# Another order of the side work in layer 2 of a four-layer kernel

## The chip, the cores and the metric

The kernel runs on one core of a Trainium2 chip, in one launch. The metric is the device time of the execution in microseconds (us). The profile names the engines PE (TensorE), DVE (VectorE), ACT (ScalarE), POOL (GpSimd) and SP (SyncE, which only issues transfers here).

## The reference, cut to what matters

Sixteen sequences of 256 tokens with 128 features go through four layers. Each adds to `x` an attention-like branch and a feed-forward branch of the same normalised input. The change is in layer 2:

```python
xn = _layernorm(x)
x = x + _L2_attn_ref(xn, ...) + _L2_ffn_ref(xn, ...)

def _L2_attn_ref(h, Wq, Wk, Wv, Wf, bf, Wo):      # "wide": 16 heads of 8, forward and backward
    q, k, v = heads(h @ Wq.T), heads(h @ Wk.T), heads(h @ Wv.T)
    f = log_sigmoid(h @ Wf.T + bf)                 # gates, cumulated along the tokens
    o_fwd = forgetting_attn(q, k, v, f)            # causal, scores + gc[q] - gc[k]
    o_bwd = flip(forgetting_attn(flip(q), flip(k), flip(v), flip(f)))
    return concat(o_fwd, o_bwd) @ Wo.T

def _L2_ffn_ref(x, ...):                           # "local": two layers l = 0, 1
    for l in range(2):
        h = shift_token(x)
        q, k, v = split(h @ wqkv[l])               # 8 heads of 64
        q, k = rotary_xpos(l2norm(q) * qs, l2norm(k) * ks)
        x = x + local_attention(q, k, v) @ wo[l]   # windows of 64 tokens
        h = layernorm(shift_token(x)) * lg + lb
        a, g = split(h @ w1[l] + b1[l])
        x = x + (a * gelu(g)) @ w2[l] + b2[l]
    return x
```

## The kernel before

The four layers run one after the other, each over 16 batches of 256 tokens; `x_all` stays in SBUF. In layer 2 a round is one pass over 24 steps, listed in `ROUND`: steps 0 to 15 are pairs of heads of the wide attention, steps 16 to 23 are pairs of heads of the local attention, four for local layer 0 and four for layer 1. Every engine runs the same program `one(rd)` over these steps. At each step PE does the scores of the step's pair (masks at L230, products at L242, or L1328 and L1337 for local pairs), then the transposes of maxima (L1430) or probabilities (L1387), weighted values (L253, L1419) and sums (L1402). DVE takes the maxima (L261 and L262, or L1725), subtracts them from the queries (L1768, `l_qm`) and normalises the sums (L1740 and L1743, L1754 and L1757). ACT takes the exponentials (L1600, L1621).

Beside this stands the rest of the work, and `BESIDE` says which items of it follow at each step, in which order. All engines go through the same list:

- ahead, for the next batch: `stats` (DVE copies `x` and does bn_stats, L1780 to L137), `norm` (L147), `xnT`, `gates` and `cumulate` (L1443, L1453; DVE writes `l_cums` at L1799), `wide_k`, `wide_q` and `wide_v` (PE L1467, L1460, L1477);
- for each local layer l: `hand` (a copy on DVE, L1814 and L1818); `hT`, only for l = 1 (PE transposes `xl` at L1319, DVE copies it out at L1771 and L1772); `qk` l i, four blocks (PE L1497, ACT squares at L1658, DVE rotates and sums at L1833 to L1841, POOL takes the power at L1573 and multiplies at L1576); `qk_t` l i (PE transposes the block, ACT copies it); `v` l c (PE L1503, ACT L1661);
- `o` l half (PE transposes, ACT copies `l_oT`, L1671), `out` l (PE L1520), `shift` and `apply` (layer norm: DVE up to L137, POOL L142, DVE L147), `normed` l, `up` and `down`, and for the wide branch `wide_o` and `wide_out` (L1487).

An engine takes the items in the order of the list and waits in its own queue. On PE, `qk` 1, `v` 1 wait until DVE has copied `hT`, and `qk_t` waits for POOL's product:

```python
b = G.fill(pe, rd, item, [("hT", )] if l == 1 else [])
...
pe.wait_ge(qkn_ready[l], n * 4 + i + 1)
```

All items with a PSUM result share ring `G` of two banks in turn: a use waits until the reader of the use before the last has taken it. The scores have rings `A` and `B`, one double bank each: PE may fill `A` again when DVE's maxima are done. Transposes, values and sums have ring `C` of two banks.

A batch's work spreads over three rounds. Rounds 0 (before), 1 (start) and 2 (second) and the last two are unrolled, with the items whose batch doesn't exist left out; 14 rounds between are one loop, whose 13 turns go back to its first instruction. In the second round and in all 14 of the loop both the items ahead and those of local layer 1 are present. SP issues two copies (`v_half`) in each local layer after the second `v`.

Of the kernel before, what the change touches and what calls it, by code (L numbers as in the profile page):

```python
# [604 lines left out]
def layer1(nc, g, B):  # L605
# [424 lines left out]


BESIDE = {
    0: [("shift", 0), ("wide_o", 0), ("wide_o", 1)],
    1: [("apply", 0), ("wide_out", )],
    2: [("normed", 0), ("qk", 0, 0)],
    3: [("o", 1, 0), ("o", 1, 1), ("qk", 0, 1), ("up", 0, 0)],
    4: [("qk", 0, 2), ("out", 1)],
    5: [("up", 0, 1), ("up", 0, 2)],
    6: [("shift", 1), ("down", 0), ("apply", 1)],
# [1 line left out]
    8: [("qk_t", 0, 0), ("up", 1, 0), ("up", 1, 1)],  # L1041
    9: [("up", 1, 2), ("qk_t", 0, 1)],
    10: [("down", 1), ("qk_t", 0, 2), ("hand", 1)],
    11: [("hand", 0), ("hT", ), ("qk_t", 0, 3), ("stats", )],
    12: [("qk", 1, 0), ("norm", )],
    13: [("v", 0, 0), ("qk", 1, 1), ("v", 1, 0)],
    14: [("qk_t", 1, 0), ("v", 0, 1), ("xnT", )],
    15: [("qk", 1, 2), ("v", 1, 1)],
    16: [("gates", ), ("qk_t", 1, 1)],
    17: [("cumulate", ), ("wide_k", 0), ("qk", 1, 3), ("qk_t", 1, 2)],  # L1050
    18: [("wide_k", 1)],
    19: [("qk_t", 1, 3), ("wide_q", 0)],
    20: [("o", 0, 0)],
    21: [("wide_q", 1)],
    22: [("o", 0, 1)],
    23: [("out", 0), ("wide_v", )],
}
AHEAD = ("stats", "norm", "xnT", "gates", "cumulate", "wide_q", "wide_k", "wide_v")
FIRST = ("qk", "v", "qk_t", "hand", "local", "o", "out")
# [1475 lines left out]
```

## Time and profile before

| | |
|---|---|
| runs | 4224.95, 4216.50, 4222.96 us; median 4222.96 |
| profiled execution, its own time | 4224.95 us |
| its span in the profile | 4222.8 us |
| granted TensorE clock, mean over the span | 0.939 |
| layer 2 in the span | about 1316 to 3190 us |

The span is what the profile covers, from its first to its last record; about 2 us of the execution lie around it. The granted clock is a share of full speed. In the rows, a line names the source line, engine, operation, output and input tile; "x4" is a count of instructions, and a matmul of this kernel's f32 data shows as two. "[0.40 <-DVE l_cums L1799]" is idle time of the engine just before, and what ended it; "issue" is an end for which the profile shows no releaser.

### The profile page before, as it was taken

The numbers are of one execution on the slowest core, as the hardware profiler recorded it, in microseconds if no ns is written. First come the engines' busy times: TensorE is split into PE (matmuls) and PEld (weight loads), VectorE is DVE, ScalarE is ACT, GpSimd is POOL, SyncE is SP. The second block draws the span as 40 slices with busy tenths as digits, with TensorE's granted clock in tenths as the row PEclk, the third lists the DMA queues.
The fourth block names the chain that finished last, engine by engine and source line by source line (L and its number), as shares of the span: only waits on it lengthen the run. The fifth ranks groups of instructions, "written<-read, shape, count | busy, mean of one in ns | idle before, by whom it ended". The sixth has DMA issues, their size and how long they took to land. (4 is left out here: it accounts for less than half of the span.)

```text
span 4222.8 us, 86111 instructions
## 1 busy us (share of the span) xinstructions
PE 3817.7 (90%) x30766; PEld 2993.4 (71%) x30766; DVE 2775.5 (66%) x7915; ACT 1878.4 (44%) x3484; POOL 645.2 (15%) x736
## 2 busy tenths in 40 slices
PE   3677999999998999999999999999978998998988
PEld 3565777777775676666666666666657887888877
DVE  2554555555554666666666666666647888888888
ACT  0001222222222455555555555555545555555555
POOL 0000000000000122212211222222212222222222
PEclk8668999999998999999999999999989999999999
DMA  5000000000000000000000000000001000000000
GB/s 131 10 7 23 0 0 0 0 0 0 0 0 36 5 9 10 9 9 9 9 9 9 9 9 9 9 9 9 9 5 47 1 2 2 1 2 2 1 2 3
DMA packets 29333, 44.63 MB, mean 11 GB/s; under 512 B 5928, under 2 KB 20816, under 8 KB 28368
## 3 DMA queue, kind: packets, MB, share of 16 engines
q1 hardware_dynamic: 29136, 41.56, 3.9%
q8 instruction: 178, 2.92, 0.3%
q14 instruction: 19, 0.16, 0.0%
HBM read 24.38 MB, written 4.19 MB: 7 GB/s over the span
## 5 line engine op out<-in xcount | busy, mean ns | idle before, releaser
L242 PE MATMUL bank<-l_kT,l_qT 32*128 32x128 f32 (+1 forms) x3072 | 407.4, 360 | 1.1
L1600 ACT ACTIVATE l_probsT<-bank 128x768 f32<-128x768 f32 x256 | 207.6, 811 | 443.3 <-PE bank L242 442.5
L142 POOL TENSOR_TENSOR l_rstd<-l_var,w_neg_half 128x2 f32<-128x2 f32 (+1 forms) x92 | 67.4, 733 | 2044.0 <-DVE l_var L137 2044.0
L242 PE MATMUL bank<-l_qm,l_kT 32*128 32x128 f32 (+1 forms) x3072 | 371.2, 335 | 0.0
L1573 POOL TENSOR_TENSOR l_rinv<-l_ssm,w_neg_half 128x8 f32<-128x8 f32 x128 | 210.2, 1642 | 731.7 <-DVE l_ssm L1841 731.6
L261 DVE TENSOR_REDUCE l_negmax<-bank 128x2 f32<-128x256 f32 (+1 forms) x384 | 197.5, 514 | 185.6 <-PE bank L242 180.5
L242 PEld LDWEIGHTS bank<-l_kT,l_qT 32*128 32x128 f32 x3072 | 227.9, 192 | 88.5 <-issue 80.8
L859 ACT ACTIVATE l_probsT<-bank 128x768 f32<-128x768 f32 x128 | 103.4, 808 | 411.4 <-PE bank L242 411.4
L230 PE MATMUL bank<-masks,ident 128*128 128x256 bf16 x1536 | 248.9, 281 | 40.8 <-issue 32.3
L2021 PE MATMUL bank<-l_xnT,w_egate 128*128 128x256 f32 x1024 | 276.4, 394 | 0.0
L2021 PE MATMUL bank<-l_xnT,w_eup 128*128 128x256 f32 x1024 | 270.1, 387 | 0.0
L2033 PEld LDWEIGHTS bank<-w_edown,l_hT 128*128 128x128 f32 x2048 | 247.5, 192 | 21.3 <-issue 15.6
L2033 PE MATMUL bank<-w_edown,l_hT 128*128 128x128 f32 x2048 | 250.5, 276 | 13.0 <-DVE l_xt L2203 13.0
L774 PE MATMUL bank<-l_xnT,w_up 128*128 128x256 f32 x1024 | 258.1, 396 | 0.0
L786 PE MATMUL bank<-w_down,l_hT 128*128 128x128 f32 x2048 | 256.0, 280 | 0.0
L242 PEld LDWEIGHTS bank<-l_qm,l_kT 32*128 32x128 f32 x3072 | 240.5, 187 | 21.2 <-issue 9.9
L786 PEld LDWEIGHTS bank<-w_down,l_hT 128*128 128x128 f32 x2048 | 244.5, 196 | 0.0
L230 PEld LDWEIGHTS bank<-masks,ident 128*128 128x128 bf16 x1536 | 151.6, 101 | 116.9 <-issue 66.5
L262 DVE TENSOR_REDUCE l_negmax<-bank 128x2 f32<-128x512 f32 (+1 forms) x384 | 228.0, 594 | 0.0
L2021 PEld LDWEIGHTS bank<-l_xnT,w_egate 128*128 128x128 f32 x1024 | 203.9, 199 | 30.2
L2209 DVE RECIPROCAL l_rden<-l_den 128x256 f32<-128x256 f32 x128 | 223.4, 1745 | 0.6
L2021 PEld LDWEIGHTS bank<-l_xnT,w_eup 128*128 128x128 f32 x1024 | 201.8, 197 | 29.6
(308 smaller groups left out, 8567.1 us busy)
## 6 DMA issues: line engine op xcount, KB each, us to landing
l_v_half<-l_v SPq DMA_DIRECT2D x32, 264.0 KB, 3.2
l_v_half<-l_v SPq DMA_DIRECT2D x32, 132.0 KB, 3.1
x_all<-in_x SPq DMA_DIRECT2D x16, 128.0 KB
w_up<-in_up SPq DMA_DIRECT2D x1, 2048.0 KB
w_down<-in_down SPq DMA_DIRECT2D x1, 2048.0 KB
scratch<-l_y SPq DMA_DIRECT2D x128, 16.0 KB
w_egate<-in_egate SPq DMA_DIRECT2D x1, 2048.0 KB, 8.4
out_x<-x_all SPq DMA_DIRECT2D x16, 128.0 KB, 1.8
```

The lines of the kernel that those rows point to most:

```text
L230: pe.matmul(diagonal(two[:, i, 0:AW]), g.ident16[:, :], diagonal(mask[:, :]), start=True, stop=False, skip_group_check=True)
L242: lasts.append(pe.matmul(bank[:, at:at + n * P], lhs[:, c * P:(c + 1) * P], rhs[:, x0 * P:(x0 + n) * P], start=False, stop=(i == 1), skip_ ...
L261: dve.tensor_reduce(negmax[:, 0, :], two[:, :, 0:s], AX.X, ALU.max, negate=True)
L262: return dve.tensor_reduce(negmax[:, 1, :], two[:, :, s:AW], AX.X, ALU.max, negate=True)
L774: last = pe.matmul(b[:, j * S:(j + 1) * S], w["up1"][:, h:h + P], xnT[:, :], start=True, stop=True)
L786: last = pe.matmul(Db[:, c * P:(c + 1) * P], hT[:, e % 2, j, c * P:(c + 1) * P], w["down1"][:, e * HC + j, :], start=(j == 0), stop=(j == ...
L859: Bt.took(act.activation(probsT[:, (u // 2) % 2, 2 * (u % 2):2 * (u % 2) + 2, :], two[:, :, 0:AW], ACT.Exp), u)
L1573: pool.tensor_tensor(rinv[:, i, :], ssm[:, i, :], g.neg_half[:, 0:LH], ALU.pow).then_inc(rinv_ready[l], 1)
L1600: Bt.took(act.activation(probsT[:, (j // 2) % 2, 2 * (j % 2):2 * (j % 2) + 2, :], two[:, :, 0:AW], ACT.Exp), rd, use)
L2021: last = pe.matmul(b[:, j * S:(j + 1) * S], wt[:, h:h + P], xnT[:, :], start=True, stop=True)
L2033: last = pe.matmul(Db[:, c * P:(c + 1) * P], hT[:, e % 2, j, c * P:(c + 1) * P], w["edown3"][:, e * HC + j, :], start=(j == 0), stop=(j == ...
L2209: dve.reciprocal(rden[:, m % 2, :], den[:, m % 2, :]).then_inc(rden_ready, 1)
```

## The change

The table `BESIDE` is the only thing edited. The same items are done, some of them at other steps or in another order within a step. Items move for all engines at once.

```diff
 BESIDE = {
-    0: [("shift", 0), ("wide_o", 0), ("wide_o", 1)],
-    1: [("apply", 0), ("wide_out", )],
-    2: [("normed", 0), ("qk", 0, 0)],
-    3: [("o", 1, 0), ("o", 1, 1), ("qk", 0, 1), ("up", 0, 0)],
+    0: [("shift", 0), ("wide_o", 0), ("wide_o", 1), ("apply", 0)],
+    1: [("wide_out", ), ("normed", 0)],
+    2: [("qk", 0, 0), ("o", 1, 0)],
+    3: [("o", 1, 1), ("qk", 0, 1), ("up", 0, 0)],
     4: [("qk", 0, 2), ("out", 1)],
...
     10: [("down", 1), ("qk_t", 0, 2), ("hand", 1)],
-    11: [("hand", 0), ("hT", ), ("qk_t", 0, 3), ("stats", )],
-    12: [("qk", 1, 0), ("norm", )],
-    13: [("v", 0, 0), ("qk", 1, 1), ("v", 1, 0)],
-    14: [("qk_t", 1, 0), ("v", 0, 1), ("xnT", )],
-    15: [("qk", 1, 2), ("v", 1, 1)],
-    16: [("gates", ), ("qk_t", 1, 1)],
-    17: [("cumulate", ), ("wide_k", 0), ("qk", 1, 3), ("qk_t", 1, 2)],
-    18: [("wide_k", 1)],
-    19: [("qk_t", 1, 3), ("wide_q", 0)],
-    20: [("o", 0, 0)],
-    21: [("wide_q", 1)],
+    11: [("hand", 0), ("stats", ), ("hT", ), ("v", 1, 0), ("norm", )],
+    12: [("qk", 1, 0), ("v", 0, 0)],
+    13: [("v", 0, 1), ("qk", 1, 1), ("qk_t", 0, 3)],
+    14: [("qk_t", 1, 0), ("v", 1, 1), ("xnT", )],
+    15: [("qk", 1, 2), ("qk_t", 1, 1)],
+    16: [("gates", ), ("qk_t", 1, 2)],
+    17: [("cumulate", ), ("qk", 1, 3), ("wide_k", 0)],
+    18: [("wide_k", 1), ("wide_q", 0)],
+    19: [("qk_t", 1, 3), ("wide_q", 1)],
+    20: [("wide_v", )],
+    21: [("o", 0, 0)],
     22: [("o", 0, 1)],
-    23: [("out", 0), ("wide_v", )],
+    23: [("out", 0)],
 }
```

## Rows read from the trace of the kernel before

**Rows 1.** The page's part 1: busy time, share of the span, instructions
```profile
PE 3817.7 (90%) x30766; PEld 2993.4 (71%) x30766; DVE 2775.5 (66%) x7915; ACT 1878.4 (44%) x3484; POOL 645.2 (15%) x736
```

**Rows 2.** Busy time by rounds of layer 2's loop; PEclk is the granted clock
```profile
2192.95:2306.82 113.87, 110.12 (x1036) 78.35 (x1037) 73.70 (x210) 62.99 (x115) 23.56 (x19) 0.94 0.04 9
...
2419.06:2527.05 107.99, 104.14 (x1036) 74.43 (x1037) 73.44 (x210) 62.99 (x115) 23.57 (x19) 1.00 0.04 9
2861.02:2977.04 116.02, 111.85 (x1036) 79.44 (x1037) 73.69 (x210) 62.99 (x115) 23.56 (x19) 0.93 0.04 9
```

**Rows 3.** PE's waits from 1440 to 3060: us in total, times, longest
```profile
PE bank L230 <- issue: 32.3, 13, 2.9
PE bank L1467 <- DVE l_cums L1799: 5.6, 14, 0.4
...
PE bank L1497 <- ACT l_oT L1671: 3.5, 14, 0.3
```

**Rows 4.** Timeline of steps 1 and 2: start, duration, instruction
```profile
2424.74 0.68 DVE L262 TENSOR_REDUCE l_negmax<-bank 128x2 f32<-128x512 f32 x1
...
2426.27 0.60 PE L230 MATMUL bank<-masks,ident 128*128 128x256 bf16 x4
```

**Rows 5.** Timeline of step 11
```profile
2471.16 0.38 PE L1319 MATMUL bank<-w_ident,l_xl 128*128 128x128 f32 x2
...
2471.37 0.60 PE L1319 MATMUL bank<-w_ident,l_qk_raw 128*128 128x128 f32 x4
...
2472.24 0.41 DVE L1771 COPY l_hT<-bank 64x256 f32<-64x256 f32 x1
...
2472.67 0.43 DVE L1772 COPY l_hT<-bank 64x255 f32<-64x255 f32 x1
...
2473.12 0.29 DVE L1780 COPY l_xn<-x_all 128x256 f32 x1
...
2474.26 0.17 DVE L137 TENSOR_SCALAR l_var<-l_mean_var 128x2 f32<-128x2 f32 x1
```

**Rows 6.** Timeline of steps 15 and 16
```profile
2488.59 1.02 PE L1497 MATMUL bank<-w_qkv,l_hT 128*128 128x512 f32 x2
...
2489.45 1.02 PE L1503 MATMUL bank<-w_qkv,l_hT 128*128 128x512 f32 x2
...
2494.02 0.64 PE L1319 MATMUL bank<-w_ident,l_qk_raw 128*128 128x128 f32 x4
2494.82 1.04 POOL L1576 TENSOR_TENSOR l_qk_raw<-l_qk_raw,l_rinv 128x512 f32<-128x512 f32 x1
```

**Rows 7.** Timeline of PE in the last full round, step 14
```profile
3127.06 1.12 PE L1319 MATMUL bank<-w_ident,l_qk_raw 128*128 128x128 f32 x4 [3.56 <-POOL l_qk_raw L1576]
3127.97 1.92 PE L1497 MATMUL bank<-w_qkv,l_hT 128*128 128x512 f32 x2
```

**Rows 8.** Timeline of PE at one turn of layer 2's loop
```profile
2524.10 0.61 PE L1477 MATMUL bank<-w_v2w,l_xnT 128*128 128x128 f32 x4
2527.05 0.39 PE L230 MATMUL bank<-masks,ident 128*128 128x256 bf16 x2 [2.34 <-issue]
```

**Rows 9.** PE's longest waits in layer 1 and in layer 3
```profile
PE bank L764 <- DVE l_negmax L262: 33.9, 16, 2.1
...
PE bank L2009 <- DVE l_kv_junk L2185: 60.7, 15, 4.1
```

**Rows 10.** Busy time and granted clock of stretches just behind waits
```profile
434.37:437.80 3.43, 3.43 (x19) 3.37 (x20) 1.30 (x3) 0.00 (x0) 0.00 (x0) 0.59 0.00 0
554.89:558.30 3.41, 3.41 (x38) 2.89 (x38) 1.91 (x5) 0.00 (x0) 0.00 (x0) 1.00 0.00 0
3253.93:3257.34 3.41, 3.41 (x9) 2.78 (x10) 3.10 (x11) 1.50 (x4) 1.10 (x2) 0.57 0.00 0
3257.34:3260.75 3.41, 3.41 (x17) 2.97 (x17) 3.19 (x6) 2.58 (x5) 0.73 (x1) 0.93 0.00 0
2192.95:2205.45 12.50, 12.41 (x77) 8.85 (x77) 6.23 (x23) 0.60 (x1) 0.70 (x1) 0.50 0.01 3
```

## The prediction

> **What bounds the kernel now.** Read the page's busy shares first: TensorE (PE) is busy 90% of the 4222.8 us span, VectorE 66% and ScalarE 44% [rows 1]. The edited table is used by layer 2 only, and there by all engines, so second comes the table of busy time by round. A full round of the loop takes 107.99 to 116.02 us. PE is busy for all but about 4 us of each, and what sets long rounds apart is not work (x1036 matmuls in each) but the granted clock: 1.00 in the shortest, 0.94 and 0.93 in the others [rows 2]. Of the 13 rounds that end in a turn of the loop, three are short and ten long, over 111 us. Third, PE's waits in layer 2 [rows 3]: 32.3 us at the turn of the loop, where the profile shows no releaser ("issue"), then, among others, 5.6 for `l_cums` (14 times 0.40) and 3.5 for `l_oT` (14 times 0.25). So the order now hides nearly every answer of the other engines under matmuls. Anything that makes PE wait is paid in full, and a reordering can give back at most the few waits of this list.
>
> So each moved item needs one question: when PE comes to it at its new place, has the other engine answered? Below I take the times of the round from 2419.06 to 2527.05, all of it at full clock.
>
> **Step 0 to 3 (`apply` 0, `normed` 0, `o` 1 0 earlier).** `apply` is 0.59 us on VectorE (L147) and now runs before step 1's maxima. Those ended at 2425.42 (L262) and would end near 2426.3; PE's masks of step 2, which need the bank, start at 2426.27 and move to 2426.5, since `normed` (0.22 us of PE) comes ahead of them [rows 4]. It just fits: cost 0. It is the first place to turn into a wait if VectorE is late. In step 3 `qk` 0 1 needs the bank of `o` 1 0, which now stands a step ahead instead of just before: the 0.25 us for `l_oT` [rows 3] go. Gain 0.25 in 14 rounds, 3.5 us.
>
> **Step 11 (`stats` ahead of `hT`, `v` 1 0 directly behind it).** This is the largest term. Before, PE transposed `xl` 1 at 2471.16, went on at 2471.37 with `qk_t` 0 3 and the scores of step 12, and first needed `hT` for `qk` 1 0 at that step's end. VectorE copied `hT` from 2472.24 to 2473.10 and only then did the statistics, 2473.12 to 2474.43 [rows 5]. Now `v` 1 0 stands directly behind `hT` on PE and reads that copy, and on VectorE the statistics stand ahead of the copy. VectorE has other work until 2472.24; then 1.31 us of statistics (2474.43 less 2473.12), then 0.86 us of copies: 2474.41, and PE is there at 2471.37. Wait: 3.04 us and a few hundredths for the release, 3.1; 1.31 of it is the statistics' place, the rest the missing cover. Behind the waiting matmul stand all of PE's queue, step 12's scores first, and behind those VectorE's and ScalarE's next inputs; they only idle along. The second round and 14 rounds of the loop have both items: 15 x 3.1 = 46.5.
>
> **Steps 15 and 16 (`qk_t` 1 1 and 1 2 a step earlier).** After `qk` 1 2 comes a chain: ScalarE's square, VectorE's rotation and sums, GpSimd's power and its product, which ends at 2495.86. The matmul began at 2488.59, so a block can be transposed 7.27 us after it [rows 6]. `qk_t` 1 2 stood at the end of step 17; it now follows `gates` in step 16, where `qk_t` 1 1 stood, at 2494.02, 5.43 us behind 2488.59. On that way `qk_t` 1 1 takes the place of `v` 1 1: four transposes (0.42, twice the 0.21 from 2471.16 to 2471.37 in rows 5) for one product (0.86, from L1497 to L1503 in rows 6), so PE is there after 5.0 us. Wait: 7.27 - 5.0 = 2.3 us, 15 times: 34.5. `qk_t` 1 1 itself stays two steps behind its `qk` and doesn't wait. The last round has little beside this chain and waits up to 3.56 us for the same product already [rows 7]; there `qk` 1 3 is now held behind `qk_t` 1 2: by that row, +4.
>
> **Step 17.** `qk` 1 3 (0.86 us) now stands between `cumulate` and `wide_k` 0 and covers the 0.40 us wait for `l_cums` [rows 3]: -6.0 in 15 rounds.
>
> **`v`, `wide_q`, `qk_t` 0 3 and 1 3, `o` 0 0.** Same instructions, other steps. Their readers are two steps or more behind, and the two banks of ring G are freed by copies such as L1772 (0.43 us, rows 5) with a product of 0.86 us between: 0. SyncE's two copies per layer half are issued no later than before, and nothing stands behind them: 0.
>
> **`wide_v`, from the last place of the round to step 20.** It is 0.6 us of PE just ahead of the turn of the loop, where PE then idles 2.34 us [rows 8]. If the next pass can begin at a time that doesn't depend on it, those 0.6 us were covered and are now in the open (13 x 0.6 = 8); if the idle time simply follows PE's last matmul, 0. Nothing decides; I take 3.
>
> **The clock.** After the turn of the loop (2.5 us idle on average) the clock stood at 0.50 (1.2 GHz, the lower of its two levels; 1.00 is 2.4 GHz) for the next 12.5 us in the round from 2192.95, and that round took 5.88 us more than the one at 1.00 [rows 2, 10]. Layer 3 waits 15 times for about 4.05 us [rows 9], and after the first of these shows 0.57 and 0.93 in two pieces of 3.41 us: 3.41 x 0.43 + 3.41 x 0.07 = 1.7 us lost [rows 10]. Layer 1 waits 16 times for about 2.1 us [rows 9], and shows 0.59 after one of them and 1.00 after another [rows 10]. So each of the two new waits costs between 0 and 5.9 us beyond itself. For step 11, with dense 128-row matmuls behind it as in layer 3, I take 1.7 (26 in all). For step 16, a wait like layer 1's but with small matmuls behind it as at a round's start, I take 2.0 (30 in all).
>
> **Sum.** 46.5 + 34.5 + 4 - 3.5 - 6 + 3 + 26 + 30 = +134.5 us on the profiled execution's 4224.95, so 4360. That execution is the slowest of three, 2 us over their median of 4222.96; against the median I say 4358.
>
> Nearest to a reason against: could PE work past the waiting matmul? The last round shows it idle for 3.56 us at L1319 with L1497 next in line [rows 7]. The Trainium skill ("TensorE: Matmul & The Clock Gate", Part 2, the step on loading weights) says that only weight loads are pulled ahead while matmuls stay in program order. By that rule the 3.1 us stand in full and the sum is 4360; were it otherwise, step 12's scores would fill them and it would be 4360 - 46.5 - 26 = 4287. The trace agrees with the rule.
>
> **Rivals.**
> 1. Both waits come, but the clock stays at 1.00 behind them, as in most of layer 1's passes: 134.5 - 56 = +78.5, so 4302 against the median. Against it: layer 3's pass in rows 10, and ten of the 13 turns of the loop.
> 2. Both come, and each brings the long low clock of a round's start: 15 x 5.9 x 2 = 177 in place of 56, so 4479. For it: step 17's matmuls are as small as those of step 0. Against it: layer 3 recovers within 7 us.
> 3. Only one wait shows, because the other's chain is shorter than I read it: without step 16, 4358 - 34.5 - 30 = 4294; without step 11, 4285.
> 4. Faster: the waits removed count and the new ones don't, because VectorE reaches `hT` before PE. The gain is 9.5 us, 4213. With a shift of the loop's turn that left the clock up in the ten rounds that lose 5 us or so it would reach 4165. It decides at the `hT` copy: it would have to end by 2471.3 where it ends at 2473.10 even in the old order. I see no row for it.
> 5. The table changes order but the waits just take other waits' places, within 0.2%.
>
> **Chances.** My forecast (4325 to 4430) 0.50; rival 1, 0.17; rival 2, 0.10; rival 3, 0.13; rival 4, 0.06; rival 5, 0.04. About 0.2% (8 us) is what a measurement of this kernel can tell from no change. Faster 0.06, same 0.04, slower 0.90. For 8 in 10 the range goes from 4280 (rivals 1 and 3 inside) to 4440.
>
> **What would show it.** Among PE's waits: L1503 for VectorE's L1772, 15 times near 3.1 us; L1319 for GpSimd's L1576, 15 times near 2.3 us; no L1467 for L1799 and no L1497 for `l_oT`. By round: 5 us more of PE idle in each, and granted clock below 1.00 in all rounds, with low stretches in the middle of the round and in its last third. I am wrong if the first wait is near 1 us or absent, if PE's clock stays up behind the waits, or if the turn of the loop changes by more than 0.5 us.

## The result, and the profile after

The changed kernel is slower by 3.5%: its median is 4365.0 us (4 runs, 4362.1 to 4377.3) against 4219.7 us (4 runs, 4208.6 to 4225.0) for the kernel before on the same chip, a ratio of 1.0353 (95% interval 1.0324 to 1.0383). The prediction said 4358 us, 4280 to 4440, slower with a chance of 0.90. The profiled execution took 4374.6 us, its span 4372.6 us; the mean granted clock is 0.920.

The page's part 1 of the kernel after, the counterpart of [rows 1]:

```profile
PE 3893.2 (89%) x30766; PEld 3038.0 (69%) x30766; DVE 2780.6 (64%) x7915; ACT 1879.5 (43%) x3484; POOL 645.6 (15%) x736
```

The instructions are the same in number. PE shows 75.5 us more busy time for the same x30766 matmuls, and its weight loads (PEld) 44.6 us more, which is the first sign that its clock was lower; DVE, ACT and POOL show 5.1 us more at most. The rest of the 149.8 us by which the span grew is PE standing idle. Its waits in layer 2 of the kernel after say where (engine, line, what it waited for: us in total, times, longest), to be set against [rows 3]:

```profile
PE bank L1503 <- DVE l_hT L1772: 46.9, 15, 3.1
PE bank L1319 <- POOL l_qk_raw L1576: 34.7, 15, 2.3
PE bank L230 <- issue: 24.5, 13, 2.1
PE bank L1419 <- ACT l_probs2T L1607: 4.5, 8, 0.6
PE bank L1319 <- DVE w_rot L1850: 4.1, 14, 0.3
PE bank L1419 <- DVE l_on L1743: 3.9, 7, 0.6
```

Two waits lead the list that weren't in it, 15 times each, and L1467 for `l_cums` and L1497 for `l_oT` are gone. One round shows both. First step 11, from the timeline of the kernel after (start, duration, instruction, and in brackets the idle time ahead of it with its releaser); it answers to [rows 5]:

```profile
1827.41 0.38 PE L1319 MATMUL bank<-w_ident,l_xl 128*128 128x128 f32 x2
...
1828.74 0.29 DVE L1780 COPY l_xn<-x_all 128x256 f32 x1 [0.16 <-DVE l_xl L1818]
...
1829.88 0.17 DVE L137 TENSOR_SCALAR l_var<-l_mean_var 128x2 f32<-128x2 f32 x1
...
1830.38 0.43 DVE L1772 COPY l_hT<-bank 64x255 f32<-64x255 f32 x1
...
1830.93 2.07 PE L1503 MATMUL bank<-w_qkv,l_hT 128*128 128x512 f32 x2 [3.14 <-DVE l_hT L1772]
```

PE issues the transpose of `xl` 1 and stands until DVE has done the statistics (1828.74 to 1829.96, when the first copy starts) and the two copies. The first product behind the wait takes 2.07 us where this kind took 1.02 us in [rows 6]: the clock is already down. Then steps 15 and 16 of the same round, from the timeline of all engines, which answers to [rows 6]:

```profile
1853.42 1.02 PE L1497 MATMUL bank<-w_qkv,l_hT 128*128 128x512 f32 x2
...
1858.00 1.64 POOL L1573 TENSOR_TENSOR l_rinv<-l_ssm,w_neg_half 128x8 f32<-128x8 f32 x1 [5.99 <-DVE l_ssm L1841]
...
1859.71 1.04 POOL L1576 TENSOR_TENSOR l_qk_raw<-l_qk_raw,l_rinv 128x512 f32<-128x512 f32 x1
...
1860.89 0.47 PE L1319 MATMUL bank<-w_ident,l_qk_raw 128*128 128x128 f32 x1 [2.31 <-POOL l_qk_raw L1576]
```

From the product of `qk` 1 2 (1853.42) to its transpose (1860.89) are 7.47 us, of which PE had work for about 5. By rounds the kernel after takes from 116.4 to 123.0 us. Here are a short round and a long one (the columns are those of [rows 2]: the stretch, its length, busy us of PE, PEld, DVE, ACT and POOL, the granted clock, DMA share and GB/s):

```profile
1659.25:1775.67 116.42, 108.15 (x1036) 76.93 (x1037) 73.88 (x210) 63.01 (x115) 23.54 (x19) 0.96 0.04 8
1775.67:1898.30 122.63, 114.49 (x1037) 80.99 (x1037) 73.96 (x210) 63.01 (x115) 23.54 (x19) 0.90 0.03 8
...
1775.67:1788.17 12.50, 12.20 (x122) 8.98 (x124) 9.45 (x31) 2.49 (x4) 0.70 (x1) 1.00 0.01 3
...
1829.80:1840.00 10.20, 9.06 (x42) 4.80 (x43) 3.01 (x9) 1.80 (x3) 0.70 (x1) 0.51 0.00 0
...
1860.50:1874.20 13.70, 13.31 (x63) 10.06 (x64) 3.81 (x12) 6.11 (x11) 0.26 (x1) 0.51 0.00 0
```

The last three rows are pieces of the round from 1775.67. The clock is at full speed behind the turn of the loop, falls at the wait of step 11, comes back (1.00 from 1848 to 1858), and falls again at the wait of step 16. Over the 12 rounds between turns, the stretch at the lower level (1.2 GHz) behind step 11 is 10.2 us long in eight and 3.4 us in four; behind step 16 it is 13.7 us in ten and 6.8 us in two. Behind none of the 13 turns is there one, although PE idles 1.88 us there on average. Before, ten of the 13 had one.

What a microsecond of the lower level costs follows from the first two rows: the long round has 13.7 us more of it (10.2 + 13.7 against 3.4 + 6.8) and is 6.2 us longer, 0.45 us for each. The first two rounds of [rows 2] give about the same: 5.88 us for a stretch of 13.7 us, 0.43 us for each.

### The profile page after: what moved, and what is told of

Its sections match the earlier page's. It is cut to its first block and busy times, and to the rows that moved or that the text cites. A ratio compares the mean times of both kernels' runs of the same rounds, so it can differ in the third digit from the quotient of the medians.

```text
span 4372.6 us, 86070 instructions
## 1 busy us (share of the span) xinstructions
PE 3893.2 (89%) x30766; PEld 3038.0 (69%) x30766; DVE 2780.6 (64%) x7915; ACT 1879.5 (43%) x3484; POOL 645.6 (15%) x736
## 5 line engine op out<-in xcount | busy, mean ns | idle before, releaser
L242 PE MATMUL bank<-l_qm,l_kT 32*128 32x128 f32 (+1 forms) x3072 | 388.6, 348 | 0.0
L242 PEld LDWEIGHTS bank<-l_qm,l_kT 32*128 32x128 f32 x3072 | 250.9, 196 | 25.4 <-issue 12.9
```

What stands on the lines that cost most here:

```text
L242: lasts.append(pe.matmul(bank[:, at:at + n * P], lhs[:, c * P:(c + 1) * P], rhs[:, x0 * P:(x0 + n) * P], start=False, stop=(i == 1), skip_ ...
```

## The experiments

Each one edits `BESIDE` of the kernel after or of the kernel before. Times are medians, ratios are to the kernel before on the same chip.

### Each wait taken away, and both

Without step 11's: `hT` ahead of `stats`, and `v` 1 0 two steps later, at the kernel after.

```diff
-    11: [("hand", 0), ("stats", ), ("hT", ), ("v", 1, 0), ("norm", )],
-    12: [("qk", 1, 0), ("v", 0, 0)],
-    13: [("v", 0, 1), ("qk", 1, 1), ("qk_t", 0, 3)],
+    11: [("hand", 0), ("hT", ), ("stats", )],
+    12: [("qk", 1, 0), ("v", 0, 0), ("norm", )],
+    13: [("qk_t", 0, 3), ("v", 0, 1), ("qk", 1, 1), ("v", 1, 0)],
```

> The changed kernel with step 11 put right: statistics behind the hT copy, v 1 0 back in step 13. Theory (each new wait costs itself and a stretch at half clock behind it): the 3.14 us wait at L1503 is gone, the 2.31 us wait at L1319 stays. By the changed kernel's rounds a microsecond at the low clock costs some 0.42 us (122.4 us with 23.9 us low, 116.4 with 10.2), so a round is some 107 + 2.3 + 5.7 (13.7 us low) = 115 us and the time about 4255. Rival (the low clock is something each round has once, wherever it falls): the stretch behind the second wait stays, and another comes back at the turn of the loop, 119 us a round and 4300.

Measured: 4252.5 us, 1.0103 (1.0081 to 1.0125). The first of its waits of PE in layer 2:

```profile
PE bank L1319 <- POOL l_qk_raw L1576: 32.3, 14, 2.3
PE bank L230 <- issue: 21.4, 13, 2.1
```

A usual round in its table of busy time by rounds:

```profile
1639.52:1752.60 113.08, 108.40 (x1036) 77.70 (x1037) 73.77 (x210) 62.87 (x115) 23.57 (x19) 0.95 0.04 9
```

The wait of step 16 stays in full (14 of its 15 lie in this window), with 3.4 to 13.7 us of low clock behind it each time. Behind the turn there is one low stretch in 12 rounds.

Without step 16's: `qk_t` 1 1 and 1 2 back, at the kernel after.

```diff
-    15: [("qk", 1, 2), ("qk_t", 1, 1)],
-    16: [("gates", ), ("qk_t", 1, 2)],
+    15: [("qk", 1, 2)],
+    16: [("gates", ), ("qk_t", 1, 1)],
     17: [("cumulate", ), ("qk", 1, 3), ("wide_k", 0)],
-    18: [("wide_k", 1), ("wide_q", 0)],
+    18: [("qk_t", 1, 2), ("wide_k", 1), ("wide_q", 0)],
```

> The changed kernel with qk_t 1 1 in step 16 and qk_t 1 2 in step 18, so that the chain of qk 1 2 is covered again; step 11 as changed. Theory: the 2.31 us wait is gone, the 3.14 us wait stays, with 3.4 to 10.2 us at the low clock behind it: 107 + 3.1 + 1.4 to 4.3 = 111.5 to 114.5 us a round, 4215 to 4250. Rival (low clock once per round at any place): also a low stretch at the turn of the loop, 117 to 119 us a round, near 4290.

Measured: 4309.8 us, 1.0242 (1.0217 to 1.0268). From its waits of PE:

```profile
PE bank L1503 <- DVE l_hT L1772: 43.8, 14, 3.1
...
PE bank L1453 <- DVE l_ze L1794: 4.7, 14, 0.3
PE bank L242 <- DVE l_qm L1768: 2.9, 14, 0.3
```

From its busy time by stretches, one of the shortest rounds and the first 10.2 us of the next:

```profile
1638.74:1754.71 115.97, 110.04 (x1036) 78.04 (x1037) 73.85 (x210) 62.71 (x115) 23.51 (x19) 0.94 0.04 8
1754.71:1764.91 10.20, 10.11 (x70) 7.13 (x71) 6.01 (x22) 0.60 (x1) 0.70 (x1) 0.55 0.01 2
```

This missed what my theory gave (4215 to 4250 us) and came nearer to its rival, low clock at the turn again and 4290 us. The wait is gone, but the low stretch at the round's start is there in all 12 rounds (10.2 or 13.7 us), though PE idles no longer at the turn than in the kernel after (1.78 us). So the clock took back much of what the wait gave. Two waits of 0.3 and 0.2 us are new as well.

Without both, the two edits together:

> Both put right, all other moves of the change kept. Theory: none of the two waits, l_cums and l_oT waits still gone, the turn of the loop idle for some 1.9 us as in the changed kernel, in place of 2.5. If the low clock at a round's start came with the longer idle time, it stays away: 107 us a round, 4150. If it only stayed away because the two waits had shifted it, it is back in most rounds: 111 us a round, 4205. Rival on the prediction (the other moves cost something too): above 4220.

Measured: 4188.5 us, 0.9942 (0.9919 to 0.9964), which is 0.6% faster than the kernel before. That lies between the two times expected, 4150 with no low start and 4205 with most. The longest of its waits of PE in layer 2's loop is the turn:

```profile
PE bank L230 <- issue: 20.6, 13, 1.7
```

Two of its rounds, one behind the other (five of 12 have a low start):

```profile
1744.27:1851.26 106.99, 103.96 (x1036) 74.20 (x1037) 73.50 (x210) 62.82 (x115) 23.60 (x19) 1.00 0.04 9
1851.26:1962.58 111.32, 108.46 (x1037) 77.51 (x1037) 73.76 (x210) 62.81 (x115) 23.59 (x19) 0.95 0.04 9
```

The whole loss is in these two waits and what hangs on them. In shares of the time before: undoing step 11 gives back 3.53% - 1.03% = 2.50% (105 us), step 16 1.11% (47 us), both 4.11% (173 us). The waits themselves are 46.9 and 34.7 us, and the last round's for POOL's product grow by 9.0 us besides (the table below); without both edits of the change they are back at 9.1 us in total, as before (9.3). The two effects don't add up (152 against 173), because with one of them gone the low clock sits elsewhere in the round.

### Half a wait

`hT` ahead of `stats`, with `v` 1 0 left where the change puts it, at the kernel after:

```diff
-    11: [("hand", 0), ("stats", ), ("hT", ), ("v", 1, 0), ("norm", )],
+    11: [("hand", 0), ("hT", ), ("stats", ), ("v", 1, 0), ("norm", )],
```

> The changed kernel with hT ahead of the statistics in step 11 again, v 1 0 still directly behind them on TensorE. It parts the 3.14 us wait: the statistics' place is worth 1.31 us, the missing cover the rest. Theory: the wait at L1503 is 3.14 - 1.31 = 1.8 us, 15 times, -20 us; whether the clock still falls behind a wait of 1.8 us decides between 4345 (it does, with stretches as before) and 4290 (it doesn't, 4 to 5 us less in each round). Rival (the wait is a fixed cost of putting v 1 0 behind hT): near 3.1 us and 4365.

Measured: 4323.7 us, 1.0252 (1.0230 to 1.0275). The first of its waits of PE:

```profile
PE bank L1319 <- POOL l_qk_raw L1576: 32.3, 14, 2.3
PE bank L1503 <- DVE l_hT L1772: 23.6, 14, 1.7
```

The wait shrinks from 3.14 to 1.69 us, by the statistics' 1.31 and a little more. Behind it the clock is low in only four of 12 rounds, where it was in all. Four rounds have a low start.

`v` 1 1 between `qk` 1 2 and its transpose again, at the kernel after:

```diff
-    14: [("qk_t", 1, 0), ("v", 1, 1), ("xnT", )],
+    14: [("qk_t", 1, 0), ("xnT", )],
     15: [("qk", 1, 2), ("qk_t", 1, 1)],
-    16: [("gates", ), ("qk_t", 1, 2)],
+    16: [("v", 1, 1), ("gates", ), ("qk_t", 1, 2)],
```

> The changed kernel with v 1 1 moved from step 14 to the head of step 16, ahead of gates: 0.86 us more of TensorE work between qk 1 2 and qk_t 1 2, nothing else. Theory: the wait at L1319 for GpSimd's product falls from 2.31 to 1.45 us, -13 us; if the low stretch behind it (13.7 us in most rounds) stays, 4352; if a wait of 1.45 us leaves the clock up, some 5 us less per round and 4275. Rival (the chain of qk 1 2 itself is held up by something in step 16): the wait stays near 2.3 us.

Measured: 4316.4 us, 1.0236 (1.0216 to 1.0257). From its waits of PE:

```profile
PE bank L1319 <- POOL l_qk_raw L1576: 18.1, 13, 1.4
```

From its table by rounds the longest, with low stretches behind the turn and both waits:

```profile
2832.44:2959.50 127.06, 119.71 (x1037) 84.53 (x1037) 74.25 (x210) 62.77 (x115) 23.54 (x19) 0.87 0.03 8
```

One product of 0.86 us as cover shortens the wait from 2.31 to 1.4 us, by 0.9. Behind it the clock stays up in nine of 12 rounds. The start is low in four. So waits of 1.4 and 1.7 us sometimes lower the clock, and waits of 2.31 and 3.14 us did each time.

### The place of `wide_v`

`wide_v` alone, at the kernel before:

```diff
-    20: [("o", 0, 0)],
+    20: [("wide_v", ), ("o", 0, 0)],
...
-    23: [("out", 0), ("wide_v", )],
+    23: [("out", 0)],
```

> The kernel before with one edit: wide_v from the end of step 23 to step 20. The prediction gave this move 0 to +8 us. The changed kernel's turns of the loop are idle for 1.9 us on average, not 2.5. If wide_v's move does that: turns near 1.9, 4212, and if the low clock needs the longer idle time, down to 4160. If the move has nothing to do with it: turns near 2.5 and 4220 to 4228.

Measured: 4206.6 us, 0.9990 (0.9978 to 1.0003). Within what can be told from no change: `wide_v`'s 0.6 us, 13 times, would be a ratio of 1.0019. PE's idle time at the turn is 26.9 us in total (2.07 on average) where before had 32.3, so it is nearer to the 1.9 us that I expected if the move shortens it than to 2.5. The other way round, `wide_v` last in the version without both waits:

```diff
-    20: [("wide_v", )],
+    20: [],
...
-    23: [("out", 0)],
+    23: [("out", 0), ("wide_v", )],
```

> The kernel with both waits put right (turn of the loop idle 1.58 us on average), with wide_v back at the end of step 23. If wide_v's place sets the idle time at the turn (code for the next pass is asked for later when more work stands ahead of it): turns near 2.0 to 2.5 us, more low starts, 4200 to 4215. If it doesn't (the idle time follows the last matmul, and its size is that of the loop's code in memory): turns stay near 1.6 us and 4185 to 4190.

Measured: 4195.8 us, 0.9959 (0.9942 to 0.9976); the idle time at the turn stays at 21.6 us in total (20.6 with `wide_v` in step 20). So `wide_v` covers nothing there. Whether its place has a part in the shorter idle time of the kernel after isn't settled: moving it at the kernel before took 5.4 of the 7.8 us away, moving it back here gave only 1.0 us back.

### The turn of the loop, with the code moved

Another candidate is where the instructions lie in the program. These two put 128 waits that are already satisfied once ahead of layer 2 on PE's queue, which moves the loop in the program (lines of their profiles are two higher behind it).

```diff
             pe.wait_ge(setup_done, 1)
+            for _ in range(128):
+                pe.wait_ge(setup_done, 1)
```

At the kernel before:

> The kernel before, with 128 waits that are already satisfied put on TensorE's queue once, ahead of layer 2's first round. The order of work is untouched; only the place of the loop's code in memory moves. So far turns of the loop idle 1.6 to 1.9 us on average in all runs whose page counts 166 packets on the instruction queue, with wide_v last or not; 2.1 us with 169, 2.5 us with 178 (the kernel before). Theory (the idle time at the turn is a matter of where the code lies): the number of packets changes and the turns with it, down to 1.6 us, 12 us less in all, or up; plus up to 5 us for the waits themselves. 4200 if it falls. Rival (the turn depends on the order of work): 2.5 us, 178 packets, 4215 to 4220.

At the kernel after:

> The changed kernel with the same 128 waits. By the same theory its turns of 1.9 us may change too (to 2.5 us if the packets go back to 178: +8 us, 4373); the two waits of 3.14 and 2.31 us can't change, nor the low stretches behind them. Rival: 1.9 us and 4365 to 4370.

Measured: 4222.5 us, 0.9992 (0.9979 to 1.0004), and 4366.0 us, 1.0346 (1.0327 to 1.0365): neither moves. The idle time at the turn is 2.35 us on average (2.48 before) and 2.01 us (1.88 in the kernel after), and in the second all waits of 3.1 and 2.3 us stay, with a low clock behind both in every round and at no turn. From the waits of PE, first of before with the code moved:

```profile
PE bank L230 <- issue: 30.5, 13, 2.7
```

And of after with the code moved:

```profile
PE bank L1505 <- DVE l_hT L1774: 40.7, 13, 3.1
PE bank L1321 <- POOL l_qk_raw L1578: 29.9, 13, 2.3
PE bank L230 <- issue: 24.1, 12, 2.4
```

Moving the code by so much doesn't turn one kernel's turn into the other's. But the traces show what goes with the idle time: transfers on the queue that the page calls q8 instruction. First the page's row of the kernel before and the row of the 5 us ahead of its turn at 2306.82, then the same of the kernel after and its turn at 1898.30 (packets, MB, share of 16 engines):

```profile
q8 instruction: 178, 2.92, 0.3%
q8 instruction: 2, 0.03, 3.8%
...
q8 instruction: 166, 2.72, 0.3%
q8 instruction: 1, 0.02, 1.5%
```

These packets have 16 KB each. Over all 169 turns of the 13 kernels, the last one ahead of a turn ends 1.5 to 2.2 us before the first matmul of the next pass. At 129 turns it is the only one, and PE idles 1.44 to 2.13 us (1.75 on average); at 40 turns there are two, and PE idles 1.66 to 3.63 us (2.45). The kernel before has two at 12 of its 13 turns, the kernel after one at all 13, and that is the whole difference of 12 in the page's count. `wide_v` alone has two at three turns; with the code moved it is 13 turns at the kernel before and nine at the kernel after. So the turn goes with these transfers, whose engine the views don't name; why an order of the items needs one or two of them stays open.

### Only the moves that should gain

At the kernel before, with steps 0 to 3 of the change:

```diff
-    17: [("cumulate", ), ("wide_k", 0), ("qk", 1, 3), ("qk_t", 1, 2)],
+    17: [("cumulate", ), ("qk_t", 1, 2), ("wide_k", 0), ("qk", 1, 3)],
-    20: [("o", 0, 0)],
+    20: [("wide_v", ), ("o", 0, 0)],
...
-    23: [("out", 0), ("wide_v", )],
+    23: [("out", 0)],
```

> The kernel before with only what should gain: apply 0, normed 0 and o 1 0 early as in the change; step 17 in the order cumulate, qk_t 1 2, wide_k 0, qk 1 3; wide_v in step 20. Theory: no l_cums and no l_oT waits (-9.5 us) and, against the run with both waits put right, no waits of 0.3 us at L1453 and 0.2 us at L242 (8 us in all there). 106.5 us in rounds at full clock, and low starts in about half of the rounds: 4175 to 4190. If the smaller idle time at the turn in the other runs (1.6 to 1.9 us) came with their wide steps and not with wide_v: turns at 2.1 to 2.5 us and 4195 to 4205.

Measured: 4192.8 us, 0.9945 (0.9927 to 0.9962). The waits for `l_cums` and `l_oT` are gone, but with `qk_t` 1 2 as their cover a new one comes in: PE at L1497, where `qk` 1 3 needs the bank of that transpose, waits for ACT's copy (L1667), 15 times up to 0.5 us. Its row among the waits:

```profile
PE bank L1497 <- ACT l_qkT L1667: 5.9, 15, 0.5
```

So the last one covers `l_cums` with `qk` 1 3, as the change does, and puts `qk_t` 1 2 a step later than before instead of a step earlier. The rest is as in the one ahead of it:

```diff
-    17: [("cumulate", ), ("wide_k", 0), ("qk", 1, 3), ("qk_t", 1, 2)],
-    18: [("wide_k", 1)],
+    17: [("cumulate", ), ("qk", 1, 3), ("wide_k", 0)],
+    18: [("qk_t", 1, 2), ("wide_k", 1)],
```

> The run with only the gains, where step 17's new order had made its own wait of 0.4 us (L1497 for l_qkT, 5.9 us in all): now cumulate, qk 1 3, wide_k 0 in step 17 as in the change and qk_t 1 2 at the head of step 18. Theory: no wait of that kind, 106.5 us in rounds at full clock, low starts in half of them: 4185. Rival: qk_t 1 2 waits for its bank (qk 1 3 is two uses back) or the clock falls at more turns: 4190 to 4200.

Measured: 4182.9 us, 0.9898 (0.9881 to 0.9915), 1.0% faster than the kernel before and, by the ratios, 4.4% faster than the kernel after. Its profiled execution is longer than that (span 4201.7 us). The turn is the first of its waits of PE in layer 2:

```profile
PE bank L230 <- issue: 28.5, 13, 3.6
```

Two of its rounds:

```profile
2408.37:2514.49 106.12, 103.65 (x1036) 74.36 (x1037) 73.43 (x210) 62.66 (x115) 23.56 (x19) 1.00 0.04 9
2853.01:2963.75 110.74, 108.17 (x1036) 77.71 (x1037) 73.72 (x210) 62.65 (x115) 23.57 (x19) 0.95 0.04 9
```

A round at full clock takes 106.12 us where the one of [rows 2] took 107.99. What is left is the turn of the loop, and the low clock behind it, which nine of its 12 rounds have.

## Why the prediction was right, and where it wasn't

The two spans differ by 149.8 us, of which 149.1 lie ahead of layer 3: its first product, L2009, starts at 3182.9 before and at 3332.0 after. Term by term:

| term | predicted | measured |
|---|---|---|
| wait of step 11 | +46.5 | +46.9 |
| wait of step 16 | +34.5 | +34.7 |
| last round | +4 | +9.0 |
| `l_oT` | -3.5 | -3.5 |
| `l_cums` | -6 | -6.0 |
| `wide_v`, the turn | +3 | -7.8 |
| other short waits of PE | 0 | +3.0 |
| clock | +56 | +73.5, what is left |
| sum | +134.5 | +149.8 |

The total came out nearer than its terms, and that is luck: the clock (17.5), the last round (5.0) and the other short waits (3.0) were taken too small, the turn (10.8) too large. Against the median it is nearer still, 4358 to 4365.0, because this profiled execution lies 9.6 us above its median.

**Step 11, step 16.** Both readings held to a few hundredths: 3.14 us where I said 3.1, 2.31 where I said 2.3, 15 times each. What made it possible is that everything ahead of the new place was known from the old order: when the producer's queue gets to the item, how long it takes, and when PE arrives. The full 3.14 us also settle the question whether PE works past a waiting matmul: here it doesn't. The first two experiments take each wait away alone. Halving them showed what they are made of: the statistics' place is 1.45 us of the wait of step 11, and one product as cover takes 0.9 us off that of step 16.

**Steps 0 to 3 and 17.** The waits for `l_oT` and `l_cums` went as said. [rows 3] end at 3060 and leave out the last of 15 waits for `l_cums`; up to 3090, where the loop's last pass has ended, the row is

```profile
PE bank L1467 <- DVE l_cums L1799: 6.0, 15, 0.4
```

`apply` 0 just fits: no wait for it is in the list. Of the items costed at nothing, a few cost tenths: `w_rot` (1.2 to 4.1 us in total) and `l_probs2T` (3.4 to 4.5), less 1.1 for `l_on` (5.0 to 3.9), together +3.0.

**Last round.** I let one of its three waits for POOL's product grow, by 4 us. All three grew. From the timelines of PE, with the wait for `hT` ahead of them, first what [rows 7] leave out of the kernel before, then the kernel after:

```profile
3118.09 3.56 PE L1497 MATMUL bank<-w_qkv,l_hT 128*128 128x512 f32 x4 [0.95 <-DVE l_hT L1772]
...
3136.32 0.66 PE L1319 MATMUL bank<-w_ident,l_qk_raw 128*128 128x128 f32 x4 [2.65 <-POOL l_qk_raw L1576]
3140.11 1.12 PE L1319 MATMUL bank<-w_ident,l_qk_raw 128*128 128x128 f32 x4 [3.13 <-POOL l_qk_raw L1576]
...
3261.29 1.12 PE L1503 MATMUL bank<-w_qkv,l_hT 128*128 128x512 f32 x2 [0.95 <-DVE l_hT L1772]
3270.17 1.12 PE L1319 MATMUL bank<-w_ident,l_qk_raw 128*128 128x128 f32 x4 [5.88 <-POOL l_qk_raw L1576]
3280.77 1.11 PE L1319 MATMUL bank<-w_ident,l_qk_raw 128*128 128x128 f32 x4 [6.00 <-POOL l_qk_raw L1576]
3290.03 1.11 PE L1319 MATMUL bank<-w_ident,l_qk_raw 128*128 128x128 f32 x4 [6.44 <-POOL l_qk_raw L1576]
```

That is 18.3 us against 3.56, 2.65 and 3.13 in the kernel before (9.3), +9.0; the wait for `hT` is the same 0.95 us in both. The term was under half of what it should have been.

**`wide_v` and the turn.** This step failed, in sign and in mechanism. I let 0 to 0.6 us per turn come into the open; PE's idle time there fell from 2.48 to 1.88 us on average instead, 7.8 us in all, a little more than the 0.5 us at which I said that I would be wrong. The other half of the choice, that the idle time simply follows PE's last matmul, has the cost right (nothing) and not the size of the idle time. That goes with the transfers of instructions ahead of the turn, two at 12 of 13 turns before and one at each after, for which the prediction had no term.

**The clock.** This step came out 17.5 us too small in its sum and wrong in its parts. I took 3.7 us per round behind the new waits on top of what the round's start loses. The low stretches behind both waits are 20.5 us per round on average, 9.2 us at 0.45 each, two and a half times that. But the start's, 9.7 us per round before (4.4 us lost), are all gone. The net is 4.8 us per round where I said 3.7. Over all of layer 2 the stretches at 0.50 add up to 372 us, before 188 us; 184 us more at 0.45 is 83 us. The table's 73.5 is lower in part because a low stretch begins while PE still waits: in the piece from 1829.80 PE is idle for the first 1.1 of 10.2 us, which costs nothing.

Why I missed the parts: layer 3's short recovery (6.8 us) was the model for step 11, and behind step 11 it took 10.2 us in two of three rounds; and I took the start's loss as a property of the start. A count is off as well: ten of the 13 turns have a low stretch and a long round behind them, but of the rounds that end in a turn nine are long and four short. No term of the sum goes by it.

**The rivals.** That the clock stays up (4302 us) falls: it fell behind every one of the new waits. That each brings a long low stretch (4479 us) was right about most stretches, and wrong in adding them to the start's. That one wait doesn't show, faster and same fall with the list of waits.

**Open.** Whether an idle time lowers the clock isn't settled by its length alone: at the turn, 1.88 us never did in the kernel after, and 1.78 us always did without step 16's wait; in the version without both waits five of 12 rounds have a low start and seven have none, behind 1.5 to 1.7 us of idle time in both cases, although nothing in the program differs from one to the next. The Trainium skill ("TensorE: Matmul & The Clock Gate", Part 1, "What's actually happening") says that the hardware's watch on activity runs freely and doesn't follow the kernel, so that the moment at which the clock changes depends on how the work falls against it. The rows agree as far as they go; no run here moves one against the other.

## What to carry to other kernels

In a loop in which one engine is busy 96% of the time, ask of each moved item only this: when the engine gets there, has the producer answered, and how many microseconds of its own work lie between? Read both from the order before; the sum was good to hundredths. Keep a producer's short copy ahead of unrelated work in its queue (the statistics ahead of `hT` cost 1.45 us per round), and price a wait on TensorE at more than its length: here 173 us for 91 us of waits, the last round's included. A mixed edit is best taken apart: its good half alone is 1.0% faster than the kernel before, the whole 3.5% slower.

## What the runs showed of the hardware

- A wait of 2.31 or 3.14 us in otherwise dense work lowered TensorE's clock every time, one of 1.4 or 1.7 us in three and four of 12 rounds. It stayed low for 3.4 to 13.7 us, at about 0.45 us lost for each microsecond.
- Low stretches don't add up over waits: with both waits in the round, the one at its start vanished; with step 16's removed it was there in all 12 rounds, with step 11's removed in one.
- PE idles at the turn of this loop for 1.4 to 3.6 us in all versions, with no releaser in the profile. Ahead of each turn stand one or two transfers of 16 KB on the instruction queue, with 1.75 and 2.45 us of idle time on average, and the last of them ends 1.5 to 2.2 us before the first matmul.
